# The first image's selective scans: half of the driving terms made on TensorE, another share of the weighing given to GpSimd

## The reference, cut to what matters

```
delta = softplus(dt)                     # one row of 1024 per channel
h[d,n,t] = exp(delta[d,t] * A[d,n]) * h[d,n,t-1] + delta[d,t] * u[d,t] * B[n,t]
y[d,t]   = sum over n of h[d,n,t] * C[n,t]
```

## Time and profile before

| | us |
|---|---|
| runs (median of 3) | 5670.45 (5668.87, 5670.45, 5677.36) |
| profiled execution: span from first to last instruction | 5675.5 |
| profiled execution: its own time | 5677.36, the only one of the three that is not shorter than the span; 1.9 us lie around the span |
| first stage, first to last scan | 45.9 to 717.3 |
| second stage, first to last scan | 889.9 to 1210.4 |

### The profile page before, as it was taken

One profiled execution on the slowest core, in us unless ns is written; L12 is line 12 of the kernel. 1 busy time (PEld: TensorE's weight loads), 2 busy tenths in 40 slices (PEclk: granted clock), 3 DMA queues, 4 the chain that ended last, 5 costly groups with the idle time before them and its releaser, 6 DMA issues. The chain is left out here.

```text
span 5675.5 us, 64660 instructions
## 1 busy us (share of the span) xinstructions
PE 4823.6 (85%) x19381; PEld 3055.2 (54%) x19381; DVE 4557.4 (80%) x4619; ACT 3512.8 (62%) x5364; POOL 4089.3 (72%) x3128
## 2 busy tenths in 40 slices
PE   6787796778989887888999988888988988888998
PEld 2232242236666645555666645555666654556777
DVE  6999947977999957996999966996999985896544
ACT  4444353337877857766887866775878765775222
POOL 6999917957999935985999953995999962984111
PEclk8898898898999999998999999998999999999999
DMA  5666405426787715645777833654778752562110
GB/s 206 230 219 229 155 21 190 156 97 244 264 280 270 267 58 179 226 164 189 273 280 262 280 119 134 217 199 151 270 267 281 259 194 79 199 225 94 42 49 28
DMA packets 341663, 1070.72 MB, mean 189 GB/s; under 512 B 31546, under 2 KB 119462, under 8 KB 334776
## 3 DMA queue, kind: packets, MB, share of 16 engines
q1 hardware_dynamic: 341304, 1066.50, 53.8%
HBM read 1052.69 MB, written 13.68 MB: 188 GB/s over the span
## 5 line engine op out<-in xcount | busy, mean ns | idle before, releaser
L1009 PE MATMUL banks<-ident,prod 128*128 128x128 f32 x4752 | 766.9, 288 | 390.4 <-DVE prod L1310 288.1
L1009 PEld LDWEIGHTS banks<-ident,prod 128*128 128x128 f32 x4752 | 561.1, 145 | 793.4 <-DVE prod L1310 549.6
L1301 DVE TENSOR_TENSOR_SCAN banks<-banks,h 128x512 f32<-128x512 f32 x594 | 723.4, 1218 | 87.3 <-ACT banks L1149 49.2
L455 PE MATMUL banks<-prod,ident 128*128 128x512 f32 x972 | 556.6, 715 | 275.9 <-DVE prod L630 212.0
L1252 POOL TENSOR_TENSOR h<-lane,Bb 128x512 f32<-128x512 f32 x576 | 723.6, 1274 | 57.1 <-DMA Bb<-half_rows 36.1
L1149 ACT ACTIVATE banks<-lane,A 128x512 f32<-128x512 f32 x864 | 581.5, 687 | 249.8 <-DVE prod L1310 82.3
L537 ACT ACTIVATE banks<-delta_first,A 128x1024 f32<-128x1024 f32 x288 | 321.2, 1117 | 517.4 <-DVE prod L630 434.1
L1081 PE MATMUL banks<-w_a,Cb 128*128 128x384 f32 x1536 | 552.6, 488 | 0.0
L455 PEld LDWEIGHTS banks<-prod,ident 128*128 128x128 f32 x972 | 198.3, 220 | 622.2 <-DVE prod L630 360.4
L1301 DVE TENSOR_TENSOR_SCAN banks<-banks,half_carry_a,h 128x512 f32<-128x512 f32 x396 | 505.8, 1277 | 9.2 <-ACT banks L1149 5.2
L1252 POOL TENSOR_TENSOR h<-half_du_a,Bb 128x512 f32<-128x512 f32 x384 | 483.1, 1276 | 15.2 <-DMA Bb<-half_rows 11.8
(11 more groups left out here) (441 smaller groups left out, 11436.1 us busy)
## 6 DMA issues: line engine op xcount, KB each, us to landing
Bb<-half_rows SPq DMA_DIRECT2D x576, 512.0 KB, 4.3
Cb<-half_rows SPq DMA_DIRECT2D x288, 512.0 KB, 4.4
w_a<-w_in SPq DMA_DIRECT2D x256, 576.0 KB, 6.1
Bb<-rows SPq DMA_DIRECT2D x144, 512.0 KB, 4.2
Cb<-rows SPq DMA_DIRECT2D x144, 512.0 KB, 3.8
w_b<-w_in SPq DMA_DIRECT2D x128, 576.0 KB, 6.1
half_C_a<-half_rows SPq DMA_DIRECT2D x128, 512.0 KB, 6.8
C_first<-rows SPq DMA_DIRECT2D x40, 1024.0 KB, 7.8
```

Source lines behind the costliest of these rows:

```text
L455: mm = eng.matmul(ps[:, c, :], m.ident[:, :], src[:, cols(c)], start=n == 0, stop=added(s) == (i + 1) * N, skip_group_check=True)
L1009: mm = eng.matmul(ps[:, 0, at], src[:, at], m.ident[:, :], start=n == 0 and k == 0, stop=added(s) == (i + 1) * N, is_transpose=True, skip_ ...
L1301: eng.tensor_tensor_scan(flip(to), flip(slot(s)), flip(m.dBu[:, s % DRIVES, :]), initial, ALU.mult, ALU.add).then_inc(st.scanned, 1)
```

## The change

All of it is in `lane_scans` and in the tensors that it gets.

- Driving terms. Those of even states stay on POOL, issued two steps ahead (`LEAD`). Those of odd states are made by PE: once in a lane PE transposes `du` (`turn_du`, 8 blocks) and ACT copies it to SBUF (`keep_du`); in each direction PE transposes the rows of B (`turn_b`), ACT copies them (`keep_b`) and builds, for each odd state and each of 8 blocks of 128 positions, a diagonal matrix (`build`, two half-builds of four copies in a state). Then 8 products of a turned block of `du` with the diagonal give the driving term in a PSUM slot.
- Decays of odd states go to a ring of four SBUF tiles (`ring`), since their slot holds the driving term; decays of even states go to the slot as before, and the even driving terms to the ring.
- Weighing: DVE keeps n = 2, 4, 6, 10, 12, 14; the other ten go to POOL, into four held tiles.
- Adding: 8 transposes of 128 by 128 in a step instead of two products of 512 columns, POOL's products three steps later (`LAG`); at the end of a lane ACT copies the sum (`copy_sum`) and PE turns it back (`back`) for `take`.
- Transfers: three tiles of B for the even states; C in a ring of four tiles, reloaded for every lane, where all sixteen rows were loaded once in a direction.
- Places: nearly all constants change, the norms go to lanes 3, 5, 6, 9, 10, 11, and a direction is projected two lanes ahead, both halves at one place (n = 11 of lanes 1, 4, 7).

```diff
-    SLOTS, DRIVES, PRODS, HELD, BRING = 2, 2, 2, 2, 4
-    PROJECT_AT, LOW_AT, STORE_AT, DT_AT = (0, 2), (4, 6), 7, 7
-    MAGNITUDE_AT, EXP_AT, LOG_AT, DELTA_AT, DU_AT = 10, 11, 12, 12, 14
-    CENTRE_AT, CENTRED_AT, SQUARE_AT, VARIANCE_AT, RSTD_AT, NORM_AT, STORE_NORM_AT = (0, 1, 3), (4, 4, 6), (6, 7, 7), 6, 9, 10, 12
+    SLOTS, RING, CRING, BRING, HELD, LEAD, LAG = 2, 4, 4, 3, 4, 2, 3
+    COPY_AT = 3
+    BACK_AT, TAKE_AT, DT_AT, MAGNITUDE_AT, LOG_AT, DELTA_AT, DU_AT = 5, 6, 7, 9, 10, 10, 11
+    PROJECT_AT, LOW_AT, STORE_AT = 11, (12, 13), 13
+    TURN_DU_AT, KEEP_DU_AT = 14, 15
+    NORM_LATER = 3
+    CENTRE_AT, CENTRED_AT, SQUARE_AT, VARIANCE_AT, RSTD_AT, NORM_AT, STORE_NORM_AT = (0, 2, 4), (2, 4, 5), (5, 6, 6), 6, 7, 8, 10
-        norm_of = {i: j for j, i in enumerate(lanes_between[:NH * len(norms.x)])}
+        norm_of = {i: j for j, i in enumerate((3, 5, 6, 9, 10, 11))}
+    OWN = (2, 4, 6, 10, 12, 14)
     def by_pool(s):
-        return s % N % 3 == 1
+        return s % N not in OWN
+    for d in range(len(directions)):
+        begin = d * TILES * N - N + 2 if d else -2
+        for k, n in enumerate(STATES):
+            for half in range(2):
+                at = begin + 2 * k + half
...
+    def vacated(eng, s):
+        if s >= SLOTS:
+            old = s - SLOTS
+            if by_pool(old):
+                eng.wait_ge(st.scanned, old + 1)
+            else:
+                eng.wait_ge(st.prod, own(old) + 1)
...
         @block.tensor
+            def turn_du(i):
+                eng.wait_ge(st.du, i + 1)
+                for k in range(TT):
+                    mm = eng.matmul(in_bank(WORK, k), m.du[:, i % 2, block_of(k)], m.ident[:, :], start=k % (HALF // P) == 0,
+                                    stop=True, is_transpose=True, skip_group_check=True)
+            def drive(s):
+                eng.wait_ge(st.du_kept, i + 1)
+                eng.wait_ge(st.diagonal, built[lanes[i].direction, n])
+                vacated(eng, s)
+                for k in range(TT):
+                    mm = eng.matmul(in_bank(2 + 2 * (s % SLOTS), k), m.du_turned[i % 2][:, block_of(k)],
+                                    diagonal(n)[:, block_of(k)], start=k % (HALF // P) == 0, stop=True, skip_group_check=True)
             def add(s):
+                if s == first_add[i]:
+                    if i:
+                        eng.wait_ge(st.copied, i)
-                for c in range(NH):
-                    mm = eng.matmul(ps[:, c, :], m.ident[:, :], src[:, cols(c)], start=n == 0,
+                for k in range(TT):
+                    mm = eng.matmul(in_bank(0, k), src[:, block_of(k)], m.ident[:, :],
...
+                                    is_transpose=True, skip_group_check=True)
...
+            for s in range(STEPS + LAG):
+                if s + 1 < STEPS and by_tensor(s + 1):
+                    drive(s + 1)
+                if s >= LAG and by_pool(s - LAG):
+                    add(s - LAG)
+                if i + 1 < len(lanes) and n == TURN_DU_AT:
+                    turn_du(i + 1)
                 if not by_pool(s):
                     add(s)
+                if n == 0 and i + 1 < len(lanes) and fresh(i + 1):
+                    turn_b(lanes[i + 1].direction)
...
         @block.scalar
+            def build(d, n, half):
+                for k in range(half * TT // 2, (half + 1) * TT // 2):
+                    ins = eng.activation(diagonal(n)[:, block_of(k)], m.ident[:, :], ACT.Copy, scale=scales(d, k, n))
+            def copy_sum(i):
+                eng.wait_ge(st.summed, all_added[i])
+                eng.activation(m.du[:, i % 2, :], flat(0), ACT.Copy).then_inc(st.copied, 1)
...
         @block.gpsimd
+            for s in range(STEPS + 1):
+                if i + 1 < len(lanes) and n == DU_AT + later(i):
+                    du(i + 1)
+                if s + LEAD < STEPS and not by_tensor(s + LEAD):
+                    drive(s + LEAD)
+                if s and by_pool(s - 1):
+                    weigh(s - 1)
```

More of the change, by code:

```diff
@@ L291, in lane_scans, with by_tensor @@
-    LANE_POOL = sum(by_pool(n) for n in range(N))
+    ring = m.ring
+    prod = m.prods
+    STATES = list(range(1, N, 2))
+    OWN = (2, 4, 6, 10, 12, 14)
+    def by_tensor(s):
+        return s % 2 == 1
+    def by_pool(s):
+        return s % N not in OWN
+    tensor_before = [0]
+    pool_before = [0]
+    for step in range(STEPS):
+        tensor_before.append(tensor_before[-1] + by_tensor(step))
+        pool_before.append(pool_before[-1] + by_pool(step))
+    pool_drives = [step for step in range(STEPS) if not by_tensor(step)]
@@ L293, in pooled, with led @@
+    def led(s):
+        return s - tensor_before[s]
     def pooled(s):
-        return s // N * LANE_POOL + sum(by_pool(n) for n in range(s % N))
+        return pool_before[s]
     def own(s):
[L299 to L306, removed]
+        return s - pool_before[s]
@@ new lines, in lane_scans @@
+    add_order = [a for b in range(STEPS + LAG) for a in ([b - LAG] if b >= LAG and by_pool(b - LAG) else []) +
+                 ([b] if b < STEPS and not by_pool(b) else [])]
+    place = {a: k + 1 for k, a in enumerate(add_order)}
+    own_steps = [step for step in range(STEPS) if not by_pool(step)]
+    pool_steps = [step for step in range(STEPS) if by_pool(step)]
+    first_add = {step // N: step for step in reversed(add_order)}
+    all_added = {step // N: place[step] for step in add_order}
@@ L402, in centre @@
                 if k == 0:
[L403 removed]
+                    eng.wait_ge(st.du_kept, i + 1)
+                    eng.wait_ge(st.b_kept, lanes[i].direction + 1)
                     eng.wait_ge(norms.st.loaded, 16 * (j + 1))
+                if k == 1 and i + 1 < len(lanes) and fresh(i + 1):
+                    eng.wait_ge(st.b_kept, lanes[i + 1].direction + 1)
                 if k == 2:
@@ new lines, in add, with back @@
+                mm.then_inc(st.summed, 1)
+            def back(i):
+                eng.wait_ge(st.copied, i + 1)
+                if i + 1 < len(lanes):
+                    eng.wait_ge(st.du_kept, i + 2)
+                if i + 2 < len(lanes) and fresh(i + 2):
+                    eng.wait_ge(st.b_kept, lanes[i + 2].direction + 1)
+                if i + 1 in norm_of:
+                    eng.wait_ge(norms.st.logged, norm_of[i + 1] + 1)
+                for k in range(TT):
+                    mm = eng.matmul(in_bank(WORK, k), m.du[:, i % 2, block_of(k)], m.ident[:, :], start=k % (HALF // P) == 0,
+                                    stop=True, is_transpose=True, skip_group_check=True)
+                mm.then_inc(st.back, 1)
@@ L472, in _ @@
                 if i in norm_of and n == VARIANCE_AT:
                     variance(i)
-                if n == DT_AT + (i in norm_of) and i + 1 < len(lanes):
+                if i and n == BACK_AT + later(i):
+                    back(i - 1)
+                if i + 1 < len(lanes) and n == DT_AT + later(i):
                     dt_product(i + 1)
+                if projects(i) and n == PROJECT_AT:
+                    for c in range(NH):
+                        project(i + 2, c)
+            back(len(lanes) - 1)
@@ L544, in _ @@
             log_of(0)
+            for what in before_first:
+                build(*what)
             for s in range(STEPS):
@@ L547, in _ @@
                 decay(s)
+                if s == 0:
+                    keep_du(0)
+                if i + 1 < len(lanes) and n == KEEP_DU_AT:
+                    keep_du(i + 1)
+                if n == 1 and i + 1 < len(lanes) and fresh(i + 1):
+                    keep_b(lanes[i + 1].direction)
+                if i and n == COPY_AT:
+                    copy_sum(i - 1)
+                for what in builds_at.get(s, ()):
+                    build(*what)
                 if turn is not None and n == 14 and i < CT:
```

327 lines of the change are left out of this document (163 added, 164 removed).

## The result

| | before | after |
|---|---|---|
| runs, median (us) | 5670.28 (4 runs, 5668.87 to 5677.36) | 5638.84 (4 runs, 5638.03 to 5643.73) |
| ratio, 95% interval | | 0.9943 [0.9931, 0.9955] |
| span of the profiled execution | 5675.5 | 5641.9 |
| first scan of the first stage | 45.86 | 52.77 |
| first stage, first scan to end of last | 671.4 | 660.7 |

The kernel is faster by 0.57%: the medians are 31.4 apart, where 49 and so 5621 were forecast. The span is 33.6 shorter: 3.8 up to the end of the first stage's scans (10.7 less 6.9), 29.8 behind that.

The account below looks back on a forecast made before the run. DVE was taken to set the pace, with POOL hardly behind. Gains of 17 us in the first stage and 32 in the second made 49, so 5621 for the median (profiled execution 5628); range 5570 to 5675.

Parts of the forecast that it names:

- Plain lanes: Lanes without a norm: DVE's instructions 45.8, 1.4 waiting kept, 0.7 for the clock; 47.9 us, 6.2 less than 54.1.
- Norm lanes: Six lanes with normalisation: ACT's in-order waits at scans 6 and 8 eat the gain; 58.4 us against 58.31 before.
- Rival 1: ACT's waits do not bite: plain lanes 47.0, norm lanes about 52.5, 95 us gained, 5575; chance 0.19.
- PE: TensorE's additions 0.86 and driving terms 1.71 each: 30.9 us a lane at full clock, well under DVE's 45.8.
- the first stage, 17 forecast: First scan stage: plain lanes gain 37, less projection and builds, norm lanes 0, less 4.8 for head and tail: 17 us.
- the tail: End of a stage: POOL's weighing, transposes, copy, turning back and take cost 1 us more than before.
- (d) head: Start of each stage: turning B 1.5, its copy 0.3, scan 1 waiting some 2.0; 3.8 us a stage.
- (c), transfers at nothing: 24 loads of 512 KB a lane, tightest C of n = 4; costed at 0, 18 us if landing takes twice as long.
- Rival 3: Plain gain eaten by jitter between POOL and PE and late loads, 3 more a plain lane; 13 us gained, 5657; chance 0.17.
- Second stage, 32 forecast: Second scan stage: six plain lanes at 6.2 gain 37, less 4.8 for head and tail: 32 us.
- Builds: ACT's half-builds meeting copy_sum and keep_du, with the turning of B: 3.0 us in each of lanes 2, 5 and 8.
- projection: Both halves at n = 11 on PE ahead of driving term 13: scan 13 2.0 us late in lanes 1, 4, 7.

Follow-up runs that it names:

- Experiment 2: Against after: ACT's take of the third centred tile stands after decay 6 instead of decay 5, with all three squares there; 5606.25 us, ratio 0.9885 to before.
- Experiment 5: Against after: additions and the turning back of a lane's sum are again 512-column products with the identity instead of transposes; 5721.24 us, ratio 1.0095 to before.
- experiment 1: Against after: the norm lanes' inverse root and normalisation one step later (after decay 8 and scan 9); 5642.38 us, ratio 0.9954 to before.
- 3: Against after: the moves of experiment 1 and Experiment 2 together; 5635.47 us, ratio 0.9934 to before.
- 10: Against 8 with the projection's second half at n = 12: second and third square behind decay 7 instead of ahead; 5606.49 us, ratio 0.988 to before.
- 8: Against 6: the normalisation issued at n = 11 instead of 10, its store at 12; 5593.55 us, ratio 0.9858 to before.
- 6: Against Experiment 2: inverse root after decay 8, normalisation at n = 10 instead of beside the take at n = 9; 5599.57 us, ratio 0.9876 to before.

## Why the prediction was right

**Plain lanes, right.** The price of 45.8 is 46.06 in the lanes where DVE waits 0.3. The six of the first stage sum to 301.8; the prediction's terms give 6 x 47.9 + 3 x 2.0 + 2 x 3.0 + 2.0 = 301.4. That they meet so closely is in part luck: the 12.6 set aside in them for old waiting and the clock stand against 6.9 lost at scan 9 and 3.4 to late C, and C was put at nothing. Those of the second came out lower, 46.1 to 48.2 beyond the first: what is lost is scan 9, 1.2 to 2.0, and nothing in two of them. POOL weighs the step between there and the window is 2.2, as the prediction had it; where scan 9 is late, driving term 9 is, though the view of waits names ACT. Two lanes of the second stage:
```profile
1058.38 3.78 PE L463 MATMUL banks<-diagonals_first,Cb 128*128 128x128 f32 x16
1106.20 2.02 PE L463 MATMUL banks<-diagonals_first,Cb 128*128 128x128 f32 x16 [0.25 <-DVE h L730]
```
The granted clock is 0.56 from 1057 to 1061, where scan 9 waits 1.96, and 1.00 from 1103 to 1108, where it does not wait. It falls here in seven of the twelve plain lanes (0.7 a lane was charged; scan 9 waits 1.1 on the mean of the twelve). PE's idle gaps ahead of it are the same in both lanes (0.50, 0.32, 0.56 and 0.19), so why it fell in one is open.

**Norm lanes, right in kind.** Waits of 4.1 at scan 6 (4.2 forecast) in all six and of 5.5 to 5.7 at scan 8 (5.4) in five, 4.0 in one, through ACT's order. The 4.2 has no full working in the prediction (5.8 less 2.2 is 3.6); in the trace the addition of step 4 starts 2.0 after its weighing, where 0.1 was counted, because driving term 5 and the addition of step 1 stand ahead of it on PE. They are 59.0 to 59.5, lane 5 with its builds 62.9, where 58.4 and 61.4 were forecast; before, norm lanes were 58.25 to 59.31. Experiment 2 gave back 33 (0.0058 of the ratio) by moving the third take and its squares: this was where the gain had gone. Rival 1 fell with that.

**PE, right.** Additions 0.87 (0.86), driving terms 1.79 (1.71), no bound, and on the mean the clock rose. The rule named there, of the Trainium skill, "TensorE: Matmul & The Clock Gate", "Part 4: PE-mode transpose", would have led to half clock; the trace differs, with 0.94 in both stages and 1.00 in a lane of little else than transposes and small products, as the earlier trace rows had it. Experiment 5 shows that without the cheap additions PE is the bound even at full clock.

**Mis-sized: the first stage, 17 forecast, 3.8 measured.** The 17 has 1.0 for the tail taken off, which lies behind the 3.8; without it 18 were forecast. Three terms make nearly all of the difference: 5.1, 5.5 and 3.1.
- *(d) head, 1.8 ahead of the first scan, measured 6.9.* PE in after, with the first product on x, the projection and the turning of B:
```profile
14.38 8.09 PE L176 MATMUL banks<-x,mean_mat 128*128 128x512 f32 x12 [14.38 <-DMA x<-x_in]
31.11 8.17 PE L419 MATMUL banks<-big,w0x 128*44 128x512 f32 x12 [3.50 <-PEq L166]
39.97 1.62 PE L429 MATMUL banks<-ident,lane 16*128 16x16 f32 x13 [0.68 <-ACT lane L568]
```
In the run of experiment 1, with the same code there:
```profile
14.13 7.62 PE L176 MATMUL banks<-x,mean_mat 128*128 128x512 f32 x12 [14.13 <-DMA x<-x_in]
30.39 5.32 PE L419 MATMUL banks<-big,w0x 128*44 128x512 f32 x12 [3.50 <-PEq L166]
```
Before, x's product began at 12.49 and lasted 7.29, the projection 5.32. From x's product to the first scan it is 33.4 before and 35.6 in experiment 1 (first scan 49.73), of which 0.3 is x's product: 1.9 is left for the change, as forecast. In after x lands 1.9 later, x's product takes 0.8 and the projection 2.85 more, and 1.4 is left. The eleven traces with this head have x's product at 12.3 to 14.4, the projection at 5.3 to 8.2 (7.0 or more in nine) and the first scan at 48.0 to 52.8, in the middle 49.1. There is one trace of before, so whether the slower projection is chance or the change is open.
- *Norm lanes*, 358.9 (the last one to the end of its last scan) against 6 x 58.4 + 3.0 = 353.4.
- *The lanes of before*, taken as 54.1 and 58.31 throughout: 674.5, while the stage is 671.4, since its last lane ends with its scan.

**Failed: (c), transfers at nothing.** DMA issues of after, first stage, as in the earlier trace rows, and the weighing of step 2 in lane 4 on DVE, with the load it waits for on SP and the weighing of step 13 of the lane before on POOL:
```profile
C_first<-rows SPq DMA_DIRECT2D x188, 512.0 KB, 5.1
Bb<-rows SPq DMA_DIRECT2D x62, 512.0 KB, 5.2
```
```profile
270.40 1.22 DVE L737 TENSOR_TENSOR prod<-banks,C_first 128x1024 f32<-128x1024 f32 x1 [1.47 <-DMA C_first<-rows]
264.56 0.38 SPq L348 DMA_DIRECT2D C_first<-rows  x1
261.28 2.36 POOL L691 TENSOR_TENSOR prod<-prod,C_first 128x1024 f32<-128x1024 f32 x1
```
A load takes 5.1, where 3.9 was counted, and the C of the first steps that DVE weighs is late six times, 8.5 in all; half the bound set for it (18). The prediction had the wrong step as the tightest. It is not n = 4, asked for 8 ahead, but five times of the six n = 2, always in the lane behind a norm lane: there (at the end of lane 3 in the lines) POOL waits 5.1 for delta, does du, a driving term and only then the weighing of n = 13; SP's queue stands 10.6 until that has freed its tile of C, and the C of n = 2, next but one behind it, is asked for 4.4 before its use and takes 5.8. No run moves `du` or adds a fifth tile of C; that the 8.5 would be gained is argued only. They lie inside the lanes counted above. Rival 3's late loads are this, at less than the 3 a lane that it had.

**Second stage, 32 forecast, 29.8 measured**: the lanes gave 37.2, but 5.6 came between the stages, where tail and head were to cost 2.8, and 1.8 after them, where a tail was to cost 1.0. The tail accounts for 0.4 and 2.5 (last scan's end to the end of the last take: 8.4 to 8.8, 6.4 to 8.9). Of the 5.6, 2.7 and 3.1 are in work that the change leaves alone: two normalisations in which PE was longer at half clock (7.25 and 7.92 for 12 records, 5.39 and 7.08 before), and a stretch told of in the last section; the head gave 0.6 back, since its projection took 10.48 against 12.17 before, without which it would have cost about 1.2. The first of the two normalisations follows right on the tail, where PE was busy 5.73 at a stretch before and is busy 1.92 and 1.97 between gaps now; whether its 1.9 belongs to the change is not shown.

**Smaller terms.** Builds 1.8 in lanes 2 and 8 (3.0), projection 2.5 (2.0), scan 1 of a stage 2.2 (2.0).

## What to carry to other kernels

When work is moved onto an engine that executes in order, write down what each wait on it holds back, and then what stands idle behind that: here the third take on ScalarE, moved by one step, gave as much again as the whole change had. A wait that is moved rather than shortened comes back at the next place with about the same price (1, 3 and 10), and a gap of over 3 us on TensorE cost twice here (1, 3 and after), once as idle time and again in the products behind it. Two engines that were relieved together can still exclude each other for single instructions: put such an instruction where the other one is waiting for it.

## What the runs showed of the hardware

**VectorE and GpSimd exclude each other in some instructions.** The normalisation, both operands in SBUF, lasts 1.73 when it starts first and the POOL operation behind it 3.7 instead of 2.36 (after, and 8); when POOL is first, it ends 1.6 after POOL's operation does, and lasts up to 3.93 (experiments 3 and 6, two lanes of 8). Scans and weighings with one operand in PSUM run beside POOL at 2.29 and 1.23. This is what the Trainium skill states in "SBUF — State Buffer", "Who interferes with whom": a VectorE instruction with two SBUF inputs contends with a GpSimd one that reads SBUF, the shared ports are an exclusive lock, and the order of issue decides who waits. The trace agrees.

**The clock fell in a stretch in which PE's records leave no gap** (their ends are modelled). PE alone in after, between the stages, where the kernel is unchanged; columns PE, PEclk, DMA, GB/s:
```profile
785.00:790.00 5.00, 5.00 (x9) 0.72 0.00 0
810.00:815.00 5.00, 5.00 (x12) 0.67 0.00 0
```
Before, the same products are at 1.00 in both windows. From the second product with kin to the projection of the second stage it is 107.3 after and 104.2 before. Just before it fell PE did products with 32 output columns and with 32 rows (780 to 788, granted 0.94 from 780 to 785). Why is open; in experiment 1 it falls at the same product (1.90 at 786.54, 1.92 at 784.55 in after, 1.04 before).
